# Last sums of a graph layer computed transposed, in blocks shifted by half a group

## The reference, cut to what matters

```python
A = corr * mask                            # correlation, kept where it is among a row's top k+1
A = 0.5 * (A + jnp.swapaxes(A, -1, -2))
A = A + jnp.eye(P, dtype=A.dtype)
deg = jnp.clip(A.sum(-1), 1e-06, None)
dinv = deg ** (-0.5)
A = dinv[..., :, None] * A * dinv[..., None, :]
...
def _rhs(A, L, theta_w, alpha_raw, x):     # L = I - A
    alpha = jnp.minimum(jax.nn.softplus(alpha_raw), 2.0)
    diff = alpha * jnp.einsum('bnpr,bnrd->bnpd', L, x)
    react = jnp.einsum('bnpr,bnrd->bnpd', A, x) @ theta_w.T
    return diff + react
...                                        # eight Runge-Kutta steps of _rhs
return jax.nn.relu(y)
```

## Time and profile before

| what | value |
|---|---|
| median of 3 runs | 1118.38 us (1118.35 to 1118.8) |
| profiled execution, own time | 1116.33 us |
| its span | 1114.5 us |
| PE busy | 1029.5 us (92%) |
| DVE busy | 743.7 us (67%) |
| ACT busy | 519.3 us (47%) |
| POOL busy | 410.6 us (37%) |
| granted TensorE clock, mean | 0.958 of full speed |

### The profile page before, as it was taken

How to read it: one execution, slowest core, us unless ns; L and a number is a source line. 1 busy time by engine, 2 the same in 40 slices (tenths; PEclk the granted TensorE clock), 3 DMA queues, 4 the chain that set the end, 5 groups by cost and what they waited for, 6 DMA issues and landing times. The chain is left out here.

```text
span 1114.5 us, 24968 instructions
## 1 busy us (share of the span) xinstructions
PE 1029.5 (92%) x9092; PEld 736.1 (66%) x9092; DVE 743.7 (67%) x3631; ACT 519.3 (47%) x1133; POOL 410.6 (37%) x555
## 2 busy tenths in 40 slices
PE   5887999999999699779999999999999999999966
PEld 4435888888887343357777777777777777777632
DVE  3685888888887323456767777676777667676353
ACT  2485777777777100124343443434344343434344
POOL 0154666666666200011332323233232333323245
PEclk8899999999999699859999999999999999999969
DMA  8000000000000000000000000000000000000033
GB/s 174 2 0 2 3 2 3 3 3 2 3 2 3 1 1 1 10 1 1 1 2 1 2 1 2 1 1 1 1 1 2 1 1 1 2 1 1 1 86 141
DMA packets 14045, 13.01 MB, mean 12 GB/s; under 512 B 3300, under 2 KB 11748, under 8 KB 13924
## 3 DMA queue, kind: packets, MB, share of 16 engines
q1 hardware_dynamic: 12548, 10.84, 3.9%
q10 hardware_dynamic: 1376, 0.59, 0.3%
HBM read 5.14 MB, written 4.19 MB: 8 GB/s over the span
## 5 line engine op out<-in xcount | busy, mean ns | idle before, releaser
L1606 PE MATMUL quad<-theta,nat 128*128 128x512 f32 x512 | 240.8, 593 | 0.0
L730 POOL TENSOR_TENSOR nat<-nat,arena 128x512 f32<-128x512 f32 x128 | 131.7, 1050 | 39.4 <-DVE arena L788 35.6
L1614 PEld LDWEIGHTS quad<-flat 128*128 128x128 f32 x768 | 104.3, 190 | 46.9 <-ACT flat L1400 24.1
L1606 PEld LDWEIGHTS quad<-theta,nat 128*128 128x128 f32 x512 | 87.5, 191 | 61.7 <-issue 61.7
L1614 PE MATMUL quad<-flat 128*128 128x128 f32 x768 | 124.7, 285 | 2.1 <-ACT flat L1400 1.0
L788 DVE CUSTOM_DVE_ANT_0 nat<-quad,arena 128x128 f32<-128x128 f32 x512 | 111.2, 282 | 1.4 <-PE quad L874 1.4
L1400 ACT ACTIVATE flat<-quad 128x256 f32<-128x256 f32 x192 | 73.5, 383 | 74.5 <-PE quad L1614 57.9
L747 ACT ACTIVATE nat<-bank 128x512 f32<-128x512 f32 x128 | 73.1, 598 | 65.3 <-PE bank L882 65.3
L1357 POOL COPY img<-flat 64x256 f32<-64x256 f32 x63 | 25.1, 399 | 186.2 <-DVE nat L1515 171.7
L882 PE MATMUL bank<-const,nat 128*128 128x128 f32 x512 | 73.3, 276 | 8.8 <-ACT nat L747 8.0
L752 ACT ACTIVATE nat<-nat 128x512 f32<-128x512 f32 x128 | 77.2, 634 | 3.8 <-POOL nat L730 3.8
(11 more groups left out here) (386 smaller groups left out, 2313.2 us busy)
## 6 DMA issues: line engine op xcount, KB each, us to landing
out<-nat SPq DMA_DIRECT2D x16, 256.0 KB, 2.0
flat<-img SPq DMA_DIRECT2D x2, 640.0 KB, 8.5
flat<-img SPq DMA_DIRECT2D x1, 512.0 KB, 4.9
const<-in_constants ACTq DMA_DIRECT2D x1, 400.5 KB, 3.2
flat<-img SPq DMA_DIRECT2D x1, 256.0 KB, 3.3
arena<-in_L_conv_Ws SPq DMA_DIRECT2D x1, 240.0 KB
nat<-in_x SPq DMA_DIRECT2D x4, 0.2 KB, 12.1
arena<-in_L_conv_Wq ACTq DMA_DIRECT2D x1, 32.0 KB, 7.0
```

What stands on the lines that cost most here:

```text
L730: pool.tensor_tensor(scored, scored, of_head(least[b], h).broadcast_to([128, ROWS, L]), ALU.subtract).then_inc(lowered, 1)
L1606: return pe.matmul(m.quad[:, n, :], vT[:, col(n)], m.theta[:, part, :], start=(part == 0), stop=False, skip_group_check=True)
L1614: last = pe.matmul(m.quad[:, row, place * C:(place + 2) * C], a8[g % 2][:, col(row)], zs[half][k % 2][:, n, :], start=False, stop=(k == 2) ...
```

## The change

The last sums change their operands. z of a row, 128 x 64, is now stationary and the fourth power moves, 128 columns, so the product has the channels on the partitions and needs no transpose. Two rows of a half fill the two halves of the partitions of bank 0 (`sum_up(f)`). The scale 1/sqrt(degree) now belongs to a column, not to a partition: POOL spreads it over 64 columns for each row (`wide`), PE turns that (`spread_scales`, into bank 1), ACT copies it to SBUF (`keep_spread`), and DVE multiplies the sums by it (`weigh_sums`, into `added`). What lies in the first columns of the `quad` banks without the last sums (the constant coefficient) is still weighed by DVE (`weigh`) and turned by PE (`turn_weighed`), and no longer waits for `sum_up`. DVE's `finish` adds the two parts, then the own term in two instructions, then ReLU and the residual.

The work is also cut anew. A window `f` holds the second half of group f - 1 and the first half of group f; there are 33 windows, the first and the last of half size. The loops have one stage more. `lay(g)` runs in stage g + 4 where it ran in stage g + 3, the ring of `yT` has six buffers where it had four, and a second buffer holds the last z of the second half (`z_last`). Some semaphores of DVE's own small steps are replaced by a shared counter (`step`), with the same waits; that part of the diff is left out, as are the buffers, the `yT` ring and the bounds of the loops.

```diff
+    def window(s):
+        f = s - 2
+        return f if 0 <= f <= GROUPS else None
+    def parts(f):
+        return [(f - 1, 1)] * (f > 0) + [(f, 0)] * (f < GROUPS)
+    def span(f):
+        return slice(0 if f > 0 else L, PAIR if f < GROUPS else L)
+    def of_part(g, half):
+        return slice((1 - half) * L, (2 - half) * L)
+    def x_window(f):
+        return m.flat[:, PAIR * f - L + span(f).start:PAIR * f - L + span(f).stop]
     with nc.Block() as block:
...
                     pool.wait_ge(laid, g)
-                pool.wait_ge(x3_ready, g + 1)
+                pool.wait_ge(x3_ready, g + 2)
                 for e in range(2):
...
                         pool.wait_ge(a2_ready, c + 1)
                 if c is not None:
+                    pool.wait_ge(square_inv_ready, 2 * (c + 1))
+                    if c >= 2:
+                        pool.wait_ge(spread_made, c)
+                    pool.tensor_copy(wide[c % 2].rearrange("p (n x) -> p n x", n=ROWS), dinv[c % 4].unsqueeze(2).broadcast_to([128, ROWS, C])).then_inc(wide_ready, 1)
                     pool.wait_ge(h4_ready, c + 1)
                     if c >= 2:
-                        pool.wait_ge(summed, 2 * (c - 1))
+                        pool.wait_ge(sum_made, c)
                     pool.tensor_tensor(quarters(a4[c % 2]), quarters(h4), square_inv.unsqueeze(2).broadcast_to([128, ROWS, L]),
...
                 kept = zs[half][k % 2]
+                if half == 0 and k == 1 and g > 0:
+                    act.wait_ge(sum_made, g)
+                if half == 1 and k == 3:
+                    act.wait_ge(sum_made, g + 1)
                 if k == 3:
-                    act.activation(kept[:, :, 0:C], m.quad[:, HALF * half:HALF * (half + 1), C:2 * C], ACT.Copy).then_inc(z_ready[half], 1)
+                    act.activation(z_last[half][:, :, 0:C], m.quad[:, HALF * half:HALF * (half + 1), C:2 * C], ACT.Copy).then_inc(z_ready[half], 1)
                 else:
...
                                    ACT.Copy).then_inc(z_ready[half], 1)
+            def keep_spread(f):
+                act.wait_ge(spread_made, f + 1)
+                if f > 0:
+                    act.wait_ge(sum_weighed, f)
+                act.activation(spread[:, span(f)], B[1][:, span(f)], ACT.Copy).then_inc(spread_ready, 1)
...
                     for k in range(3):
+                        if k == 2:
+                            keep_spread(c)
                         keep_z(c, 0, k)
...
                             keep_z(c, 1, k)
-            act.wait_ge(x3_ready, GROUPS)
+            keep_spread(GROUPS)
+            act.wait_ge(x3_ready, GROUPS + 1)
             act.activation(m.cols3[:, :, ROWS * LAST:GROUPS * ROWS:2].rearrange("p j t -> p t j"), of_half(LAST, 0), ACT.Copy)
...
         def _(dve):
+            step = m.chain(dve, "dve")
             def weigh(g, half):
-                dve.wait_ge(summed, 2 * g + half + 1)
-                if g > 0:
-                    dve.wait_ge(final_made, g)
+                dve.wait_ge(z_ready[half], 4 * g + 4)
+                if g + half > 0:
+                    dve.wait_ge(final_made, g + half)
                 dve.tensor_tensor(weighed[half].rearrange("p (n x) -> p n x", n=HALF), m.quad[:, HALF * half:HALF * (half + 1), 0:C],
...
-            def finish(g):
-                dve.wait_ge(final_made, g + 1)
-                dve.scalar_tensor_tensor(out=held, in0=yT[g % 4], scalar=m.c0[:, :], in1=B[3][:, 0:PAIR],
-                                         op0=ALU.mult, op1=ALU.add).then_inc(held_ready, 1)
-                dve.wait_ge(held_ready, g + 1)
-                dve.scalar_tensor_tensor(out=x_of(g), in0=held, scalar=0.0, in1=x_of(g),
+            def weigh_sums(f):
+                cols = span(f)
+                dve.wait_ge(sum_made, f + 1)
+                dve.wait_ge(spread_ready, f + 1)
+                if f > 0:
+                    dve.wait_ge(held_ready, f)
+                dve.tensor_tensor(added[:, cols], B[0][:, cols], spread[:, cols], ALU.mult).then_inc(sum_weighed, 1)
+            def finish(f):
+                cols = span(f)
+                dve.wait_ge(final_made, f + 1)
+                dve.wait_ge(sum_weighed, f + 1)
+                step(dve.tensor_tensor(held[:, cols], added[:, cols], B[3][:, cols], ALU.add))
+                for g, half in parts(f):
+                    at = of_part(g, half)
+                    last = dve.scalar_tensor_tensor(out=held[:, at], in0=yT[g % DEEP][:, half * L:(half + 1) * L], scalar=m.c0[:, :],
+                                                    in1=held[:, at], op0=ALU.mult, op1=ALU.add)
+                last.then_inc(held_ready, 1)
+                dve.wait_ge(held_ready, f + 1)
+                dve.scalar_tensor_tensor(out=x_window(f), in0=held[:, cols], scalar=0.0, in1=x_window(f),
                                          op0=ALU.max, op1=ALU.add).then_inc(x3_ready, 1)
...
                 p, c, r, a = stage(s)
+                f = window(s)
                 if c is not None:
...
                     weigh(r, 0)
+                if f is not None:
+                    weigh_sums(f)
                 if p is not None:
...
                     last.then_inc(xs_ready, 1)
-                if r is not None:
-                    finish(r)
-                    dve.wait_ge(x3_ready, r + 1)
-                    dve.bn_stats(m.stats[:, 6 * r:6 * r + 6], x_of(r))
-                    dve.tensor_reduce(m.rowsum[:, HALF * r:HALF * (r + 1)], x_of(r).rearrange("p (t j) -> p t j", t=HALF), AX.X, ALU.add)
+                if f is not None:
+                    finish(f)
+                    dve.wait_ge(x3_ready, f + 1)
+                    if f > 0:
+                        dve.bn_stats(m.stats[:, 6 * (f - 1):6 * f], x_of(f - 1))
+                        dve.tensor_reduce(m.rowsum[:, HALF * (f - 1):HALF * f], x_of(f - 1).rearrange("p (t j) -> p t j", t=HALF), AX.X, ALU.add)
             dve.wait_ge(laid, GROUPS - 1)
...
-            def sum_up(g, half):
-                pe.wait_ge(z_ready[half], 4 * g + 4)
-                for n in range(HALF):
-                    row = HALF * half + n
-                    last = pe.matmul(m.quad[:, row, 0:C], a4[g % 2][:, col(row)], zs[half][1][:, n, 0:C],
-                                     start=False, stop=True, skip_group_check=True)
-                last.then_inc(summed, 1)
+            def spread_scales(f):
+                pe.wait_ge(wide_ready, min(f + 1, GROUPS))
+                pe.wait_ge(v34_ready, min(f + 1, GROUPS))
+                for g, half in parts(f):
+                    last = pe.transpose(B[1][:, of_part(g, half)], wide[g % 2][:, half * L:(half + 1) * L], ident)
+                last.then_inc(spread_made, 1)
+            def sum_up(f):
+                if f + 1 < GROUPS:
+                    pe.wait_ge(h2_ready, f + 2)
+                else:
+                    pe.wait_ge(a8_ready, GROUPS)
+                if f > 0:
+                    pe.wait_ge(sum_weighed, f)
+                for g, half in parts(f):
+                    pe.wait_ge(z_ready[half], 4 * g + 4)
+                    for n in range(HALF):
+                        last = pe.matmul(B[0][n * C:(n + 1) * C, of_part(g, half)], z_last[half][:, n, 0:C], a4[g % 2][:, col(HALF * half + n)],
+                                         start=True, stop=True, skip_group_check=True)
+                last.then_inc(sum_made, 1)
+            def turn_weighed(f):
+                pe.wait_ge(weighed_ready, min(2 * f + 1, 2 * GROUPS))
+                if f + 2 < GROUPS:
+                    pe.wait_ge(cor_ready, f + 3)
+                elif f > 0:
+                    pe.wait_ge(held_ready, f)
+                for g, half in parts(f):
+                    last = pe.transpose(B[3][:, of_part(g, half)], weighed[half], ident)
+                last.then_inc(final_made, 1)
...
             LAST = GROUPS - 1
                 p, c, r, a = stage(s)
+                f = window(s)
                 if s == 0:
...
                         horner(r, 1, 0)
-                    sum_up(r, 0)
                 if p is not None:
                     pe.wait_ge(xsT_ready, p + 1)
-                    if r is not None and r > 0:
-                        pe.wait_ge(held_ready, r)
+                    if f is not None and f > 0:
+                        pe.wait_ge(held_ready, f)
                     for t in range(HALF):
...
                     kind_weights()
+                if f is not None:
+                    sum_up(f)
                 if c is not None:
...
                 if c is not None:
+                    if f is not None:
+                        pe.wait_ge(sum_weighed, f + 1)
                     square(a2, h2).then_inc(a4_made, 1)
...
                     for t in range(HALF):
                     last.then_inc(y_turned, 1)
+                if f is not None:
+                    turn_weighed(f)
                 if s == -1:
...
                     theta(1, v12T, 0)
-                if r is not None:
```

(44 more changed lines are left out.)

20 lines of the change are left out of this document (10 added, 10 removed).

## The result

| | before | after |
|---|---|---|
| median of the runs taken together, us | 1118.37 (1117.38 to 1118.8) | 1131.78 (1131.46 to 1134.12) |
| profiled execution, own time | 1116.33 | 1131.49 |
| its span | 1114.5 | 1129.7 |

Each median is of four runs. The ratio is 1.0126, with a 95% interval from 1.0109 to 1.0142: the change costs 1.3%. The forecast was 1132.2 us.

What follows compares the result with a forecast made beforehand. PE, busy 92% of the span, bounds the kernel. -0.38 + 0.22 + 0.50 = +0.34 us a stage, +10.5 us over 31 stages, plus 3.3 at the layer's end, +13.8: 1132.2 us against the median, range 1122 to 1139.

Steps and rivals of the forecast that it cites:

- The added wait: PE before the first half's Horner step 3: ACT copies the scales before the third z copy, +0.50 us a stage.
- The last sums: On PE, four matmuls with swapped operands take 0.51 us instead of 0.89: -0.38 us a stage.
- The transposes: On PE behind Horner step 2, two new transposes of the scales: +0.22 us a stage; the moved pair changes nothing.
- The work costed at nothing: Some 0.9 us a stage of added DVE work, POOL's spreading copy and PE's other new waits: all hidden, 0 us.
- The end: At the third layer's end, POOL's `lay(30)` waits for window 31: +3.3 us, bounds 1.5 and 5.
- Rival (a): Horner step 3 does not start later, ACT's idle time absorbing the scales' copy: -2.2 us, 1116.2 us; chance 0.10.
- rival (b): ACT's copies do not overlap and transposes cost 0.38, or layer end costs 5: up to 1142 us, chance 0.13.
- Rival (c): New sums alternate between two output blocks, so four cost 0.90 us and the swap saves nothing: 1144 us, chance 0.04.

Runs made afterwards that it cites:

- the scales turned early: Changed kernel with the scales' two transposes moved forward on PE, ahead of the last coefficients, and ACT's copy ahead of the degrees' square root: 1123.3 us, ratio 1.0045.
- the gap-filled kernel: Changed kernel with ACT's scales copy behind the third z copy and the weighed pieces' transposes moved between Horner steps 2 and 3: 1118.2 us, ratio 1.0000.
- the added copy: Changed kernel with one more DVE copy of 256 columns into an unread buffer ahead of ReLU in finish: 1136.0 us, ratio 1.0149.

## Why the prediction was right

- **The added wait** was put at +0.50 us a stage and measured +0.49, on the place and by the engines named. The experiment that moves one copy takes 0.48 of it away. This step is shown.
- **The last sums** were put at -0.38; the table gives -0.44 and +0.01 in the two stretches where they stood, -0.43 together. From start to start the sums themselves went from 0.89 to 0.49 us (799.85 to 800.34). The products behind the old and the new place became 0.05 us shorter each (v12 0.97 us at 800.34, from 1.02), and the Horner step ahead of the correlations 0.06 longer (0.56 us at 798.65, from 0.50); these neighbours were not in the sum. The factor of up to two of the Trainium skill, TensorEngine Tiling (Array Packing), Theoretical Speedup, would have meant -0.445. The measured -0.43 is nearer to it than to the -0.38 of the row, and doubling the sums gives 0.44 us for four.
- **The transposes**: +0.22 forecast, +0.21 measured, but at another place than the prediction said. It charged the new pair (the scales, in the gap behind Horner step 2) and took the moved pair (the weighed pieces) for free. The table and the scales turned early show the reverse: a pair costs 0.21 to 0.22 us in PE's full stretches and nothing in the gap, which held two pairs before and after. The sum came out because one pair was added in all. That is luck: had the new pair joined the others in the gap, as in the gap-filled kernel, this term would have been nearly nothing (the gap took 1.10 us with three pairs).
- **The work costed at nothing** was mine to miss in one point. DVE's added instructions are hidden, as the added copy shows. POOL's copy is hidden by the trace, not by an experiment: in the stages of the changed kernel the fourth power is weighed 1.9 us before it is used. But I only asked whether new work on DVE fits, not whether PE, having become faster between the v12 products and theta(2), runs into what it waits for there. It does: the graph's transposes wait for POOL behind the top-k chain, and the stretch grew by 0.07 us; copying the correlations first takes the same 0.07 away. This nearly cancels the 0.05 us that the sums gained over the forecast, so the stage came out at +0.33 for +0.34. That it agrees to a hundredth is two misses against each other, and luck.
- **The end**: +3.3 forecast (its own terms add up to 3.2), +3.2 measured, set by POOL as said, since `lay(30)` now waits for window 31. Inside it two misses cancel. Measured from the last v12 products, the last sums start 0.8 us later and not 0.5 (16.42 for 15.63 us): in the last group, step 2 of the second half also stands ahead of the scales' transposes in the written order, and PE waits 0.75 us before step 3. POOL's stretch, taken as unchanged, was 0.3 us shorter.
- Rival (a), the wait absorbed, fell: ACT's idle time lies ahead of the transposes. Of rival (b) nothing was needed: the copies overlap as before. Rival (c) fell with the row of L1699, 0.49 us where it wanted 0.90, and with the doubled sums.
- The span grew by 15.2 us for 13.8 forecast; 1.3 us of that came ahead of the first v12 products and say nothing on the change.

## What to carry to other kernels

Swapping the operands of a narrow matmul nearly halved it here (0.89 to 0.49 us a stage), but look where its new helpers stand on the in-order engines: one copy ahead of the wrong neighbour cost more (15 us) than the shorter sums gained (13 us), and the added pair of transposes took half of that gain as well (7 us). When PE is the bound, measure the chain times between its dependent steps: work put into such a gap was free here until it was full, the same work elsewhere cost its full length. And once PE gets faster, find the next chain under it before expecting the gain; here the best version (1108.9 us, 0.8% under the kernel before) needed the swap, the filled gap and an earlier start of the DVE chain together.

## What the runs showed that I had not expected

The second chain lay only 0.3 us under PE's own 7.51 us in the kernel before, though PE showed no wait for it and was busy for 99.7% of the time there. It can be read from DVE's rows of the kernel before, the start of the chain and its end:

```profile
795.52 0.87 DVE L1522 MAX8 arena<-nat 128x8 f32<-128x128 f32 x4 [2.16 <-ACT nat L1436]
...
800.18 0.28 DVE L1493 TENSOR_TENSOR flat<-quad,arena 128x128 f32<-128x128 f32 x1
```

The weighing ends at 800.46, 7.19 us behind the v12 products (793.27), and theta(2) starts at 800.78. The chain cost something only once PE was made faster. And four of the swapped sums beside eight matmuls of their form cost 0.44 us, 0.11 each, not the 0.13 that the eight alone show.
